# An eight-core transformer layer: tail transposes and half of the next layer norm issued ahead of the output projection

## The chip, the cores and the metric

The kernel runs on one Trainium2 chip, on all 8 of its cores at once, each core with one of the 8 sequences of the batch. No core speaks to another. The metric is the device time in microseconds (us) of the slowest core.

## What is computed

One layer with adaptive layer norms, on x of shape 8 x 2048 x 1024, 16 heads, and 8 experts:

```python
h = layernorm(x) * (1 + ca) + sa              # sa, ca, ga, sb, cb, gb come from silu(c) @ wmod
Q, K, V = h @ wq + bq, h @ wk + bk, h @ wv + bv
Q, K, V = (t.reshape(B * 16, 2048, 64) for t in (Q, K, V))
ctx = softmax(Q @ K.T / 8) @ V
out = ctx.reshape(B, S, E) @ wo + bo + h
x = x + ga * (layernorm(out) * gamma + beta)
h = layernorm(x) * (1 + cb) + sb
p = softmax(h @ gate_w + gate_b);  p = p * (p >= 0.1);  p = p / sum(p)
x = x + gb * sum_e p[:, e] * (h @ expert_w[e] + expert_b[e])
```

The reshape takes the heads from rows, not from columns: a head is made of 128 whole rows of the projections, so 256 rows hold two complete heads. Attention over them needs nothing of the other rows.

## The kernel before

The 2048 rows of a core are cut into 8 **octets** of 256 rows (two tiles of 128, i = 0 and 1). The loop at line 683 takes one octet after the other, and each is a fixed sequence that is written out by hand; every engine has one queue of instructions in order, and semaphores tie the queues together. In an octet come:

1. The rest of the first layer norm (lines 700 to 734). For each tile, VectorE turns the normalised rows that lie in `Kasm` into h: times CAb (L707), plus SAb (L710) in fp32 in `hf32`, and a bf16 copy into `h_bf` (L713). Then TensorE transposes the 8 blocks of 128 columns of `hf32` (L726) into two PSUM places of `pbD` in turn, and VectorE copies each to `hT` (L731). `hf32` holds one tile, so the second tile's h waits for the first one's transposes.
2. Q and K projections into `pbA` (L754), read out by VectorE into `Qasm` and `Kasm` (L764, L769), V projections into `pbB` and `pbC` (L804, read out by L812).
3. Attention (lines 827 to 953): four passes of 16 steps; a step is two score matmuls (L878), an exponential on ScalarE (L889), two matmuls with V (L851), and two matmuls whose result nobody reads (L897, L903). Between passes the context is scaled into `ctxFM` (L934, L939, L943). In the first three passes VectorE and ScalarE also run parts of the chain of the octet before (`chain_stage`: second and third layer norm), whose stage 4 leaves the first tile of h2 in `hf32`.
4. When the last pass is read out, GpSimd issues a transfer within SBUF that brings half of `ctxFM` to the lower 64 partitions (L949, the **context shift**), and behind it the load of the next octet's wq (L480). The output projection (L967, L974) waits for the shift: 36 matmuls, first into `pbA`, then into `pbB`. VectorE adds `h_bf` and writes `preLN` (L982).
5. The **tail** of the octet before (`emit_tail_transposes`, not in octet 0): 16 transposes of h2 (L598) with 16 copies to `h2T` (L605); between the 8th and the 9th, VectorE makes h2 of the second tile (L574, L578).
6. The **gate** of the octet before (`emit_gate_tail`): per tile, small matmuls (L623, L633, L674) and some 14 small VectorE instructions in a chain (L630 to L678).
7. The **first part of the next octet's layer norm** (`emit_ln1_pair`): statistics, two small ScalarE operations and the normalised rows into `Kasm` (L401 to L417), for both tiles; then the loads of the next weights are put in GpSimd's queue. The load into `wbuf1` waits for the output projection, which reads it.

Octet 0 has neither 5 nor 6, octet 7 has no 7. Behind the loop, the tail and the gate of octet 7 follow, then the experts. Semaphore `v1` counts VectorE's instructions, `t1`, `m1`, `m2` and `t2` count TensorE's; `pbd_guard` holds back the next octet's L897 until all of `v1` up to the octet's end is reached. A helper (`Prog.emit`) puts a drain ahead of each VectorE and ScalarE instruction that reads what the same engine has just written, or that counts a semaphore.

Of the kernel before, what the change touches and what calls it, by code (L numbers as in the profile page):

```python
# [13 lines left out]
BF16 = mybir.dt.bfloat16  # L14
# [6 lines left out]
DM = 1024  # L21
NB = 16
NOCT = 8
# [76 lines left out]
def build_program():  # L100
# [28 lines left out]
    CAb = sb("CAb", [128, DM], BF16)  # L129
    SAb = sb("SAb", [128, DM], BF16)  # L130
# [43 lines left out]
    P = Prog(nc, sems, None)  # L174

    for tt in range(NB):
        P.emit("sync", lambda e, tt=tt: e.dma_start(
            xsb[:, DM * tt:DM * (tt + 1)], x_h.ap()[128 * tt:128 * (tt + 1), :]),
            inc="dx", inc_n=16)
# [4 lines left out]
        inc="dsc", inc_n=16)  # L184
# [192 lines left out]
    h_bf = sb2("h_bf", [128, 2 * DM], BF16)  # L377
# [44 lines left out]
    ln1_sv = {}  # L422

# [11 lines left out]
    if True:  # L435
# [32 lines left out]
        emit_ln1_pair(0)  # L468
        P.flush_block()
# [19 lines left out]
    TAILT1 = {}  # L489
# [193 lines left out]
    for oct_ in range(NOCT):  # L683
        if True:
# [15 lines left out]
            for i in range(2):  # L700
                tt = 2 * oct_ + i
                hw = [ln1_sv[oct_][i]]
                if i == 0 and oct_ >= 2:
                    hw.append(("t1", TAILT1[oct_ - 2]))
                if i == 1:
                    hw.append(("t1", P.val("t1")))
                P.emit("vector", lambda e, i=i: e.tensor_mul(  # L707
                    hf32[:, 0:DM], Kasm[:, DM * i:DM * (i + 1)], CAb[:, :]),
                    waits=hw, writes=("hf",))
                P.emit("vector", lambda e, i=i: e.tensor_add(  # L710
                    hf32[:, 0:DM], hf32[:, 0:DM], SAb[:, :]),
                    reads=("hf",), writes=("hf",), inc="v1")
                P.emit("vector", lambda e, i=i: e.tensor_copy(  # L713
                    h_bf[:, DM * i:DM * (i + 1)], hf32[:, 0:DM]),
                    reads=("hf",), inc="v1")
                hdone_i = P.val("v1")
# [238 lines left out]
        if True:  # L955
            pso0 = pbA[:, :]
# [24 lines left out]
            for i in range(2):  # L981
                P.emit("vector", lambda e, i=i: e.tensor_add(  # L982
                    preLN[:, DM * i:DM * (i + 1)], pso[i][:, :],
                    h_bf[:, DM * i:DM * (i + 1)]),
                    waits=[("m2", m2v[i])], writes=("pl%d" % i,), inc="v1")
                PLV[(oct_, i)] = P.val("v1")
            if oct_ >= 1:
                emit_tail_transposes(oct_ - 1, recip_copied)
                emit_gate_tail(oct_ - 1)
            if oct_ + 1 < NOCT:  # L990
                emit_ln1_pair(oct_ + 1)
                load_weight(oct_ + 1, 0)
                load_weight(oct_ + 1, 1)
# [129 lines left out]
```

How the kernel before makes its waits and increments, by code:

```python
            def run(eng):  # L76
                for fn, waits, inc, inc_n in ops[eng_name]:
                    for s, v in waits:
                        eng.wait_ge(sems[s], v)
                    ins = fn(eng)
                    if inc is not None:
                        ins.then_inc(sems[inc], inc_n)
```

## Time and profile before

| | us |
|---|---|
| median of 3 runs | 2604.74 |
| lowest, highest | 2585.26, 2699.93 |
| profiled execution, its own time | 2597.9 |
| span of its slowest core (core 2) | 2596.4 |
| spans of the other cores | 2568.4 to 2588.5 |
| TensorE busy on core 2 | 1843.8 |
| VectorE busy on core 2 | 903.1 |
| mean granted TensorE clock, core 2 (share of 2.4 GHz) | 0.820 |

The span runs from the first to the last instruction of a core; the 1.5 us between it and the execution's own time lie around it. Octets lie between 318 and about 2048 us of the span, the experts behind 2100 us. Numbers with an L are lines of the kernel, names with an arrow are what an instruction writes and reads, and "idle before" names what ended the idle time of the engine ahead of a row. The granted clock is 0.50 at 1.2 GHz and 1.00 at 2.4 GHz.

### The profile page before, as it was taken

The numbers are of one execution on the slowest core, as the hardware profiler recorded it, in microseconds if no ns is written. First come the engines' busy times: TensorE is split into PE (matmuls) and PEld (weight loads), VectorE is DVE, ScalarE is ACT, GpSimd is POOL, SyncE is SP. The second block draws the span as 40 slices with busy tenths as digits, with TensorE's granted clock in tenths as the row PEclk, the third lists the DMA queues.
The fourth block names the chain that finished last, engine by engine and source line by source line (L and its number), as shares of the span: only waits on it lengthen the run. The fifth ranks groups of instructions, "written<-read, shape, count | busy, mean of one in ns | idle before, by whom it ended". The sixth has DMA issues, their size and how long they took to land.

```text
span 2596.4 us, 23765 instructions; the slowest of 8 cores (2568.4 to 2596.4 us)
## 1 busy us (share of the span) xinstructions
PE 1843.8 (71%) x7658; PEld 725.2 (28%) x7658; DVE 903.1 (35%) x1481; ACT 719.3 (28%) x692; POOL 42.4 (2%) x78
## 2 busy tenths in 40 slices
PE   0131189688668849948874993897588379999994
PEld 0000042242232223213222321422322124444441
DVE  2432130242262053134216214322620553333336
ACT  0000026327307504712640660363076000000000
POOL 0000000000000000000000000000000000000000
PEclk9855588789879868878886986978798569999997
DMA  8625730120120112012011101201200031112203
GB/s 235 194 89 95 187 115 1 69 74 1 69 73 1 37 35 71 1 69 73 1 56 54 34 1 69 73 1 69 73 1 4 1 66 33 33 33 51 47 1 130
DMA packets 41837, 150.48 MB, mean 58 GB/s; under 512 B 15597, under 2 KB 15597, under 8 KB 37112
## 3 DMA queue, kind: packets, MB, share of 16 engines
q0 software_dynamic: 20480, 96.51, 13.8%
q1 hardware_dynamic: 21240, 52.46, 6.3%
q8 instruction: 68, 1.11, 0.2%
q14 instruction: 49, 0.40, 0.1%
HBM read 151.09 MB, written 16.78 MB: 65 GB/s over the span
## 4 chain that ended last, share of the span: by engine, by line
PE 56%; DVE 12%; ACT 8%; issue 5%; DMA 4%; DVEq 2%; ACTq 1%; POOLq 0%; SPq 0%
PE pbA L1061 9%; PE pbC L851 9%; PE pbB L1061 9%; PE pbD L897 6%; PE pbA L878 5%; PE pbB L878 5%; ACT hT L889 4%; PE pbA L754 3%; PE pbD L903 2%; PE pbD L726 2%; PE pbA L967 2%; DVEq L54 2%; DMA Kasm<-Kasm 2%; DVE recipB L934 2%; ACT recipB L919 1%
## 5 line engine op out<-in xcount | busy, mean ns | idle before, releaser
L889 ACT ACTIVATE hT<-pbA,cm,c 128x1024 bf16<-128x1024 f32 x256 | 308.2, 1204 | 480.3 <-PE pbA L878 476.3
L851 PE MATMUL pbC<-hT,Vbuf 128*65 128x512 bf16 x1024 | 340.6, 418 | 39.6 <-ACT hT L889 37.7
L889 ACT ACTIVATE hT<-pbB,cm,c 128x1024 bf16<-128x1024 f32 x256 | 308.1, 1204 | 108.6 <-PE pbB L878 103.3
L934 DVE CAST recipB<-pbD 64x1024 bf16<-64x1024 f32 x32 | 38.9, 1216 | 812.5 <-PE pbD L929 812.5
L1061 PE MATMUL pbA<-We,h2T 128*128 128x512 bf16 x1024 | 234.2, 382 | 1.8 <-DVE facc L1034 1.8
L897 PE MATMUL pbD<-CAb 128*128 128x512 bf16 x512 | 217.9, 426 | 22.4 <-DVE recipB L934 22.4
L1061 PE MATMUL pbB<-We,h2T 128*128 128x512 bf16 x1024 | 231.5, 379 | 0.0
L878 PE MATMUL pbB<-Qasm,Kasm 64*128 64x512 bf16 x512 | 172.0, 420 | 0.0
L878 PE MATMUL pbA<-Qasm,Kasm 64*128 64x512 bf16 x512 | 169.2, 414 | 2.8 <-DMA Kasm<-Kasm 2.8
L754 PE MATMUL pbA<-hT,wbuf 128*128 128x256 bf16 x1024 | 145.2, 293 | 20.9 <-DVE Qasm L769 7.4
L903 PE MATMUL pbD<-CAb 128*128 128x256 bf16 x512 | 150.3, 294 | 0.0
L726 PE MATMUL pbD<-identf,hf 128*128 128x128 f32 x128 | 53.6, 444 | 129.6 <-DVE h_bf L713 120.8
L1061 PEld LDWEIGHTS pbA<-We,h2T 128*128 128x128 bf16 x1024 | 100.7, 98 | 125.4 <-issue 6.2
L1061 PEld LDWEIGHTS pbB<-We,h2T 128*128 128x128 bf16 x1024 | 100.1, 98 | 121.0
L851 PEld LDWEIGHTS pbC<-hT,Vbuf 128*65 128x65 bf16 x1024 | 104.6, 119 | 104.6 <-issue 79.9
L1069 DVE SCALAR_TENSOR_TENSOR facc<-pbA,w_gate,facc 128x1024 bf16<-128x1024 f32 x64 | 82.2, 1284 | 143.7 <-PE pbA L1061 143.7
L1069 DVE SCALAR_TENSOR_TENSOR facc<-pbB,w_gate,facc 128x1024 bf16<-128x1024 f32 x64 | 82.2, 1284 | 138.5 <-PE pbB L1061 138.5
L897 PEld LDWEIGHTS pbD<-CAb 128*128 128x128 bf16 x512 | 49.6, 97 | 272.2 <-issue 272.2
L283 PE MATMUL pbA<-macc,onescol 128*1 128x512 f32 x24 | 14.1, 720 | 153.1 <-DVEq L271 147.3
L754 PEld LDWEIGHTS pbA<-hT,wbuf 128*128 128x128 bf16 x1024 | 99.5, 104 | 66.7 <-issue 48.8
L598 PE MATMUL pbD<-identf,hf 128*128 128x128 f32 x128 | 46.5, 387 | 66.7 <-DVE hf L578 45.6
L646 ACT ACTIVATE gatee<-gatef,stats 128x8 f32<-128x8 f32 x16 | 4.8, 301 | 300.1 <-DVE stats L642 300.1
(162 smaller groups left out, 1468.2 us busy)
## 6 DMA issues: line engine op xcount, KB each, us to landing
wbuf<-wbh POOLq DMA_DIRECT2D x32, 2048.0 KB, 9.0
wmstage<-wmod SPq DMA_DIRECT2D x32, 768.0 KB, 4.9
We<-ew POOLq DMA_DIRECT2D x8, 2048.0 KB, 13.7
xsb<-x SPq DMA_DIRECT2D x16, 512.0 KB, 13.0
wbh<-wbuf SPq DMA_DIRECT2D x4, 2048.0 KB, 13.3
out<-xsb SPq DMA_DIRECT2D x16, 512.0 KB, 2.6
wbuf<-wq POOLq DMA_DIRECT2D x1, 2048.0 KB, 15.6
wbuf<-wk POOLq DMA_DIRECT2D x1, 2048.0 KB, 35.6
```

Of the source, the lines that this page charges most:

```text
L54: self.ops[eng].append((lambda e: e.drain(), (), None, 0))
L726: P.emit("tensor", lambda e, cch=cch, par=par: e.transpose(pst[par][:, :], hf32[:, 128 * cch:128 * (cch + 1)], identf[:, :]), waits=tw, in ...
L754: P.emit("tensor", lambda e, wtile=wtile, fo=fo, fc=fc, par=par: e.matmul(psq[par][:, :], wtile[:, DM * fc + 128 * fo:DM * fc + 128 * (fo ...
L851: P.emit("tensor", lambda e, h01=h01, gp=gp, q4=q4, par=par: e.matmul(psc[:, 512 * q4:512 * (q4 + 1)], vview[:, h01, gp, 0:65], PT[:, 1024 ...
L878: P.emit("tensor", lambda e, h01=h01, q2=q2, gp=gp, q4=q4, par=par: e.matmul(pss[par][:, 512 * q4:512 * (q4 + 1)], Kasm[0:64, T * h01 + 12 ...
L889: P.emit("scalar", lambda e, par=par: e.activation(PT[:, 1024 * par:1024 * (par + 1)], pss[par][:, :], AF.Exp, bias=cm3[:, :], scale=c0125 ...
L897: P.emit("tensor", lambda e: e.matmul(pbD[:, 0:512], CAb[:, 0:128], CAb[:, 0:512], start=True, stop=True), waits=fw)
L903: P.emit("tensor", lambda e: e.matmul(pbD[:, 0:256], CAb[:, 0:128], CAb[:, 0:256], start=True, stop=True), inc=("m1" if gp == 15 else None))
L934: P.emit("vector", lambda e: e.tensor_copy(recipB[0:64, :], psr[:, :]), waits=[("t2", tv)], writes=("recipB",), inc="v1")
L967: P.emit("tensor", lambda e, i=i, ec=ec, hh=hh: e.matmul(pso[i][:, 512 * hh:512 * (hh + 1)], cview[:, 0, ec, i, :], wbuf1[:, DM * ec + 512 ...
L1061: P.emit("tensor", lambda e, e_i=e_i, tt=tt, fc=fc, hh=hh, par=par: e.matmul(pse[par][:, 512 * hh:512 * (hh + 1)], h2T[:, T * fc + 128 * t ...
L1069: P.emit("vector", lambda e, e_i=e_i, tt=tt, par=par: e.scalar_tensor_tensor(facc[:, DM * tt:DM * (tt + 1)], pse[par][:, :], w_gate[:, NEX ...
```

## The change

Three things move, and nothing is added or dropped in number.

- The tail of the octet before (part 5) is issued ahead of the output projection instead of behind it, on TensorE and on VectorE.
- The first part of the next octet's layer norm (part 7) is issued behind the tail and ahead of the `preLN` additions.
- The h of the next octet's first tile (L707, L710, L713 for i = 0) leaves the start of the next octet. A new function, `emit_h0`, issues it directly behind the first part of the layer norm; for octet 0 it stands at the end of the block that prepares the weights. As it writes `h_bf` while the current octet's first tile there is still to be read, `h_bf` gets a third slot, and the first tile alternates between slots 0 and 2.

The gate (part 6) and the weight loads stay behind the `preLN` additions.

```diff
--- before.py
+++ after.py
@@ -374,7 +374,8 @@
     wbuf0 = sb2("wbuf0", [128, NFC * DM], BF16)
     wbuf1 = sb2("wbuf1", [128, NFC * DM], BF16)
     wbuf = (wbuf0, wbuf1)
-    h_bf = sb2("h_bf", [128, 2 * DM], BF16)
+    h_bf = sb2("h_bf", [128, 3 * DM], BF16)
+    h0slot = lambda o: (o % 2) * 2 * DM
     xnscr = sb2("xnscr", [128, 2 * DM], BF16)
     sqscr = xnscr
     preLN = sb2("preLN", [128, 2 * DM], BF16)
@@ -420,6 +421,22 @@
         return ("v1", P.val("v1"))
 
     ln1_sv = {}
+    HD0 = {}
+
+    def emit_h0(o, extra_t1=None):
+        hw = [ln1_sv[o][0]]
+        if extra_t1 is not None:
+            hw.append(("t1", extra_t1))
+        P.emit("vector", lambda e: e.tensor_mul(
+            hf32[:, 0:DM], Kasm[:, 0:DM], CAb[:, :]),
+            waits=hw, writes=("hf",))
+        P.emit("vector", lambda e: e.tensor_add(
+            hf32[:, 0:DM], hf32[:, 0:DM], SAb[:, :]),
+            reads=("hf",), writes=("hf",), inc="v1")
+        P.emit("vector", lambda e, o=o: e.tensor_copy(
+            h_bf[:, h0slot(o):h0slot(o) + DM], hf32[:, 0:DM]),
+            reads=("hf",), inc="v1")
+        HD0[o] = P.val("v1")
 
     def emit_ln1_pair(o):
         svs = []
@@ -466,6 +483,7 @@
         P.emit("vector", lambda e: e.tensor_copy(borow_bf[:, :], rowB[:, 0:DM]),
                reads=("rowBB",), inc="v1")
         emit_ln1_pair(0)
+        emit_h0(0)
         P.flush_block()
 
     slot_free = {0: None, 1: None}
@@ -699,21 +717,20 @@
             P.emit("vector", lambda e: e.memset(vview[:, :, :, 64:65], 1.0))
             for i in range(2):
                 tt = 2 * oct_ + i
-                hw = [ln1_sv[oct_][i]]
-                if i == 0 and oct_ >= 2:
-                    hw.append(("t1", TAILT1[oct_ - 2]))
                 if i == 1:
-                    hw.append(("t1", P.val("t1")))
-                P.emit("vector", lambda e, i=i: e.tensor_mul(
-                    hf32[:, 0:DM], Kasm[:, DM * i:DM * (i + 1)], CAb[:, :]),
-                    waits=hw, writes=("hf",))
-                P.emit("vector", lambda e, i=i: e.tensor_add(
-                    hf32[:, 0:DM], hf32[:, 0:DM], SAb[:, :]),
-                    reads=("hf",), writes=("hf",), inc="v1")
-                P.emit("vector", lambda e, i=i: e.tensor_copy(
-                    h_bf[:, DM * i:DM * (i + 1)], hf32[:, 0:DM]),
-                    reads=("hf",), inc="v1")
-                hdone_i = P.val("v1")
+                    hw = [ln1_sv[oct_][1], ("t1", P.val("t1"))]
+                    P.emit("vector", lambda e: e.tensor_mul(
+                        hf32[:, 0:DM], Kasm[:, DM:2 * DM], CAb[:, :]),
+                        waits=hw, writes=("hf",))
+                    P.emit("vector", lambda e: e.tensor_add(
+                        hf32[:, 0:DM], hf32[:, 0:DM], SAb[:, :]),
+                        reads=("hf",), writes=("hf",), inc="v1")
+                    P.emit("vector", lambda e: e.tensor_copy(
+                        h_bf[:, DM:2 * DM], hf32[:, 0:DM]),
+                        reads=("hf",), inc="v1")
+                    hdone_i = P.val("v1")
+                else:
+                    hdone_i = HD0[oct_]
                 ev0 = P.val("v1")
                 for cch in range(NFC):
                     k = i * NFC + cch
@@ -953,6 +970,12 @@
             V_EXP_LAST = exp_done[63]
 
         if True:
+            if oct_ >= 1:
+                emit_tail_transposes(oct_ - 1, recip_copied)
+            if oct_ + 1 < NOCT:
+                emit_ln1_pair(oct_ + 1)
+                emit_h0(oct_ + 1,
+                        extra_t1=(TAILT1[oct_ - 1] if oct_ >= 1 else None))
             pso0 = pbA[:, :]
             pso1 = pbB[:, :]
             pso = (pso0, pso1)
@@ -979,16 +1002,15 @@
                 m2v[i] = P.val("m2")
             slot_free[1] = ("m2", P.val("m2"))
             for i in range(2):
-                P.emit("vector", lambda e, i=i: e.tensor_add(
+                hcol = DM if i == 1 else h0slot(oct_)
+                P.emit("vector", lambda e, i=i, hcol=hcol: e.tensor_add(
                     preLN[:, DM * i:DM * (i + 1)], pso[i][:, :],
-                    h_bf[:, DM * i:DM * (i + 1)]),
+                    h_bf[:, hcol:hcol + DM]),
                     waits=[("m2", m2v[i])], writes=("pl%d" % i,), inc="v1")
                 PLV[(oct_, i)] = P.val("v1")
             if oct_ >= 1:
-                emit_tail_transposes(oct_ - 1, recip_copied)
                 emit_gate_tail(oct_ - 1)
             if oct_ + 1 < NOCT:
-                emit_ln1_pair(oct_ + 1)
                 load_weight(oct_ + 1, 0)
                 load_weight(oct_ + 1, 1)
             pbd_guard = P.val("v1")
```

On VectorE, at the end of octet 2, the queue before runs from the last context scaling (L943) to the gate's first copy (L630):

```order
L939 TENSOR_TENSOR ctxFM<-pbC,recipB 64x4x128
L943 TENSOR_TENSOR ctxFM<-pbC,recipB 64x4x128
L982 TENSOR_TENSOR preLN<-pbA,h_bf 128x1024
L982 TENSOR_TENSOR preLN<-pbB,h_bf 128x1024
L605 CAST h2T<-pbD 128x128 x8
L574 TENSOR_TENSOR hf<-xnscr,CBb 128x1024
L578 TENSOR_TENSOR hf<-hf,SBb 128x1024
L605 CAST h2T<-pbD 128x128 x8
L630 COPY gEM<-pbC 8x128
```

In the changed kernel (its line numbers are larger: L960 is the last scaling, L623 the copies to `h2T`, L592 and L596 h2) the same place goes on with the tail and the layer norm's statistics:

```order
L960 TENSOR_TENSOR ctxFM<-pbC,recipB 64x4x128
L623 CAST h2T<-pbD 128x128 x8
L592 TENSOR_TENSOR hf<-xnscr,CBb 128x1024
L596 TENSOR_TENSOR hf<-hf,SBb 128x1024
L623 CAST h2T<-pbD 128x128 x8
L402 BN_STATS stats<-xsb 128x6
```

Ten rows of the layer norm further on, VectorE comes to `emit_h0` (L430 to L436), to the `preLN` additions (L1006) and to the gate (L648):

```order
L418 TENSOR_SCALAR Kasm<-xsb,stats 128x1024
L430 TENSOR_TENSOR hf<-Kasm,CAb 128x1024
L433 TENSOR_TENSOR hf<-hf,SAb 128x1024
L436 CAST h_bf<-hf 128x1024
L1006 TENSOR_TENSOR preLN<-pbA,h_bf 128x1024
L1006 TENSOR_TENSOR preLN<-pbB,h_bf 128x1024
L648 COPY gEM<-pbC 8x128
```

So the additions, which stood first, now stand behind 31 instructions that do not need the output projection, and the gate follows them at once. At the border of two octets VectorE's queue before was:

```order
L417 TENSOR_SCALAR Kasm<-xsb,stats 128x1024
L699 MEMSET Vbuf 128x32
L707 TENSOR_TENSOR hf<-Kasm,CAb 128x1024
L710 TENSOR_TENSOR hf<-hf,SAb 128x1024
L713 CAST h_bf<-hf 128x1024
L731 CAST hT<-pbD 128x128 x8
```

and it is now, from the gate's last rows on:

```order
L687 TENSOR_SCALAR w_gate<-gatee,stats 128x8
L696 CAST wT_bf<-pbC 8x128
L717 MEMSET Vbuf 128x32
L748 CAST hT<-pbD 128x128 x8
L722 TENSOR_TENSOR hf<-Kasm,CAb 128x1024
```

Nothing stands any more between the gate and the copies of the first tile's transposes but a memset. On TensorE the end of an octet before was (L929 belongs to the attention, L967 and L974 are the output projection):

```order
L929 MATMUL pbD<-recipB,onesb 64x512 x2
L967 MATMUL pbA<-wbuf,ctxFM 128x512 x16
L974 MATMUL pbA<-borow_bf,ones1b 128x512 x2
L967 MATMUL pbB<-wbuf,ctxFM 128x512 x16
L974 MATMUL pbB<-borow_bf,ones1b 128x512 x2
L598 MATMUL pbD<-identf,hf 128x128 x16
L623 MATMUL pbC<-h2T,gw_bf 8x128 x8
```

and it is now (L946 is the attention's row, L616 the tail's transposes, L990 and L997 the output projection, L641 the gate's first matmuls):

```order
L946 MATMUL pbD<-recipB,onesb 64x512 x2
L616 MATMUL pbD<-identf,hf 128x128 x16
L990 MATMUL pbA<-wbuf,ctxFM 128x512 x16
L997 MATMUL pbA<-borow_bf,ones1b 128x512 x2
L990 MATMUL pbB<-wbuf,ctxFM 128x512 x16
L997 MATMUL pbB<-borow_bf,ones1b 128x512 x2
L641 MATMUL pbC<-h2T,gw_bf 8x128 x8
```

The 16 transposes now stand between the attention and the output projection. On ScalarE the two small operations per tile of the layer norm now come ahead of the gate's two exponentials. The queues of GpSimd and SyncE keep their order.

## Rows read from the trace of the kernel before

**Rows 1.** Part 1 of the page: busy us, share of the span, instructions.
```profile
PE 1843.8 (71%) x7658; PEld 725.2 (28%) x7658; DVE 903.1 (35%) x1481; ACT 719.3 (28%) x692; POOL 42.4 (2%) x78
```

**Rows 2.** Timeline of core 2, 898 to 962 us: start, length, engine, line, names, count, idle before.
```profile
897.84 0.68 DVE L943 TENSOR_TENSOR ctxFM<-pbC,recipB 64x512 bf16<-64x512 f32 x1
...
902.34 6.26 PE L967 MATMUL pbA<-wbuf,ctxFM 128*128 128x512 bf16 x16 [6.67 <-DMA ctxFM<-ctxFM]
...
909.06 3.63 PE L967 MATMUL pbB<-wbuf,ctxFM 128*128 128x512 bf16 x16
...
913.33 1.22 DVE L982 TENSOR_TENSOR preLN<-pbB,h_bf 128x1024 bf16<-128x1024 f32 x1 [2.87 <-PE pbB L974]
914.71 0.29 DVE L605 CAST h2T<-pbD 128x128 bf16<-128x128 f32 x1 [0.16 <-issue]
...
925.08 0.29 DVE L605 CAST h2T<-pbD 128x128 bf16<-128x128 f32 x1 [0.17 <-PE pbD L598]
926.74 0.28 DVE L630 COPY gEM<-pbC 8x128 f32<-8x128 f32 x1 [1.37 <-PE pbC L623]
...
937.89 0.28 DVE L678 CAST wT_bf<-pbC 8x128 bf16<-8x128 f32 x1 [0.62 <-PE pbC L674]
938.09 0.67 DVE L401 BATCH_NORM_STATS2 stats<-xsb 128x6 f32<-128x512 f32 x1
...
944.11 0.81 DVE L417 TENSOR_SCALAR Kasm<-xsb,stats 128x1024 bf16<-128x1024 f32 x1
...
947.51 0.69 DVE L713 CAST h_bf<-hf 128x1024 bf16<-128x1024 f32 x1
948.91 0.29 DVE L731 CAST hT<-pbD 128x128 bf16<-128x128 f32 x1 [0.70 <-PE pbD L726]
...
952.33 0.29 DVE L731 CAST hT<-pbD 128x128 bf16<-128x128 f32 x1 [0.16 <-PE pbD L726]
...
960.72 1.65 PE L754 MATMUL pbA<-hT,wbuf 128*128 128x256 bf16 x7 [0.76 <-DVE hT L731]
```

**Rows 3.** Stretches of core 2: length; busy PE, PEld, DVE, ACT, POOL; clock; DMA share; GB/s.
```profile
898.50:902.30 3.80, 0.00 (x0) 0.00 (x0) 0.02 (x1) 0.00 (x0) 1.08 (x2) 0.50 0.60 129
913.20:925.50 12.30, 5.54 (x17) 2.39 (x16) 8.34 (x19) 0.00 (x0) 0.53 (x1) 0.69 0.47 172
```

**Rows 4.** Timeline of core 2, weight loads of the output projection.
```profile
903.14 0.15 PEld L967 LDWEIGHTS pbA<-wbuf,ctxFM 128*128 128x128 bf16 x1 [0.28 <-issue]
903.57 0.15 PEld L967 LDWEIGHTS pbA<-wbuf,ctxFM 128*128 128x128 bf16 x1 [0.28 <-issue]
```

**Rows 5.** Timeline of core 2's VectorE, end of octet 0 and start of octet 1.
```profile
491.00 0.68 DVE L943 TENSOR_TENSOR ctxFM<-pbC,recipB 64x512 bf16<-64x512 f32 x1
...
502.75 1.22 DVE L982 TENSOR_TENSOR preLN<-pbA,h_bf 128x1024 bf16<-128x1024 f32 x1 [11.06 <-PE pbA L974]
...
506.84 1.22 DVE L982 TENSOR_TENSOR preLN<-pbB,h_bf 128x1024 bf16<-128x1024 f32 x1 [2.87 <-PE pbB L974]
...
518.81 0.29 DVE L731 CAST hT<-pbD 128x128 bf16<-128x128 f32 x1 [0.70 <-PE pbD L726]
```

**Rows 6.** Timeline of core 2's VectorE in octet 7.
```profile
2007.10 0.68 DVE L943 TENSOR_TENSOR ctxFM<-pbC,recipB 64x512 bf16<-64x512 f32 x1
...
2036.39 0.28 DVE L630 COPY gEM<-pbC 8x128 f32<-8x128 f32 x1 [1.37 <-PE pbC L623]
```

**Rows 7.** Stretches of core 0: attention of octet 0, then of octet 5.
```profile
368.10:486.30 118.20, 103.29 (x417) 35.23 (x424) 10.32 (x12) 87.00 (x73) 0.00 (x0) 0.96 0.00 1
1426.70:1559.10 132.40, 117.02 (x416) 36.18 (x424) 23.83 (x34) 87.63 (x80) 0.00 (x0) 0.84 0.00 1
```

**Rows 8.** Answer for line 949, the context shift.
```profile
DMA to landing us min/median/max: 2.8/2.9/3.4
```

**Rows 9.** Answer for line 480, the weight loads from scratch.
```profile
DMA to landing us min/median/max: 7.9/9.0/14.0
```

## The prediction

> **What bounds the kernel now.** I read the page's busy times first. No engine fills the span: TensorE is busy 71% of it, VectorE 35%, ScalarE 28% [rows 1]. So the time is a chain through several engines, and the question is which stretches are serial. The list of cores came next (all within 28 us, clocks 0.820 to 0.832): every core tells the same story. Then I took the timeline of one border between two octets, from the last context scaling of octet 2 to the first Q projection of octet 3 [rows 2]. It lasts from 898.52 (897.84 + 0.68) to 960.72, that is 62.2 us, and it is one chain:
>
> - 3.8 us in which TensorE and VectorE stand, until the context shift lands at 902.3 [rows 2, 3];
> - the output projection and the last `preLN` addition, to 914.55;
> - the tail, first copy 914.71, last copy ending 925.37: 10.66 us;
> - the gate, to 938.17: 11.43 us from its first copy at 926.74, ahead of which TensorE's first gate matmuls take 1.37 us;
> - the layer norm's first part, 938.09 to 944.92: 6.83 us;
> - h of the first tile, to 948.20: 3.28 us;
> - eight transposes and their copies, 948.91 to 952.62: 3.71 us;
> - the same for the second tile (h, then transposes), 8.10 us to 960.72.
>
> In each item one engine waits for the other. Nothing of the next octet's attention can start before it ends, so every microsecond taken from this chain is a microsecond of the run. The border stands seven times in the program, six times in this form (octets 1 to 6) and once without tail and gate (octet 0); octet 7 has the projection, the tail and the gate.
>
> **Octets 1 to 6, step by step.** I count t from the end of the last scaling (898.52 before). The tail needs only octet-old data: h2 of its first tile has been in `hf32` since the third attention pass.
>
> 1. VectorE copies the tail's blocks out from t = 0.16 on, and is through at 0.16 + 10.66 = 10.8. TensorE's last transpose ends some 0.4 us earlier, at 10.4. The shift still lands at 3.8, under this work, so its wait vanishes; but the projection, which began at 3.8, now begins at 10.4.
> 2. The projection took from 902.34 to 913.2, 10.9 us [rows 2]: its `pbA` half took 6.26 us with the clock at first at 1.2 GHz, its `pbB` half 3.63 us at 2.4. I keep 10.9, as the clock was at 0.50 behind the attention [rows 3] and will be again, so it ends at 21.3.
> 3. Beside it VectorE does the layer norm's first part, 10.8 + 6.83 + some 0.1 = 17.7, and h of the first tile, 17.7 + 3.28 = 21.0. Both `preLN` additions follow (1.22 us and a gap each): 23.6. The second one could have started at 21.4, so VectorE is the later by 0.9 us. This is the new bound of the step, and it is nearly a tie.
> 4. The gate's first matmuls run on TensorE behind the projection, from 21.3 to 22.5, under the additions. The gate then needs its 11.43 us from 23.7: 35.1.
> 5. The transposes of the next first tile wait for nothing more than TensorE. The copies begin at 35.3 and take 3.71: 39.0. The rest is unchanged, 8.1: 47.1.
>
> The gain is 62.2 - 47.1 = 15.1 us at each of six borders, 90.6. It is less than the 6.83 + 3.28 + 10.66 us that move, since the projection lost its early start: what really vanishes is the shift's 3.8 us and the overlap of two 10 us pieces.
>
> **Octet 0.** There the projection begins when it did. VectorE's 10.1 us of layer norm and h fit in front of the first addition, which came 11.1 us after the last scaling (502.75 against 491.68) and can come there still [rows 5]. From the end of the second addition (508.06) to the first copy of the next transposes (518.81) stand 10.75 us [rows 5], of which a gap of 0.16 stays: gain 10.6.
>
> **Octet 7.** From the last scaling (2007.78) to the gate's first copy (2036.39) are 28.6 us [rows 6]. After: projection from 10.4 to 21.3, second addition to 22.7 (no layer norm holds VectorE), copy at 22.8. Gain 5.8. The gate and all behind it stay.
>
> **The start.** h of tile 0 moves ahead of a barrier between blocks instead of behind it, on the same chain; the weight loads leave the barrier with only 3.71 + 8.10 = 11.8 us of transposes and h [rows 2] between them and the first Q matmul. The median load takes 9.0 us, the slowest 14.0 [rows 9], and the one that Q reads is the first of the two. Zero, at worst 2.2 us.
>
> **Sum.** 90.6 + 10.6 + 5.8 = 107.0 us. Against the profiled execution, 2597.9 - 107.0 = 2490.9. The median shown is 2604.74, 7 us above it, and the lowest run 2585.26, 13 us below; I stay with 2491.
>
> What is nothing in this sum, and its cover: the third slot of `h_bf` is only an address. The load into `wbuf1` is issued when the projection ends, 10 us later against the shift, at t = 21.8; with 14.0 us for the slowest [rows 9] it lands at 36, and the K projection that reads it comes some 10 us after 47. If it took twice as long, the wait would still be none. The attention's own work is untouched.
>
> The cost that the trace does not show is VectorE's copies running while the shift is issued by GpSimd. Lower bound nothing; upper bound the 9.0 us that the large loads need in place of the shift's 2.9 [rows 8, 9], so 6.1 us later. At octets 1 to 7 the projection has 6.6 us of slack behind the shift and takes nothing; at octet 0 it costs at most 6.1. I take zero, as the shift's own row is the nearer one.
>
> The Trainium skill ("SBUF — State Buffer", section "Who interferes with whom") has a rule that speaks against this: a transfer issued by GpSimd waits for its descriptors while VectorE runs in a two-port mode, which copies and tensor_scalar between SBUF tiles can take. The tail's copies read PSUM and by the same page do not, so by this rule only octet 0, where the layer norm runs beside the shift, could lose. No run here shows it yet.
>
> **Rivals.**
>
> *The projection runs at 1.2 GHz throughout.* For it: beside the tail's transposes the clock fell to a mean of 0.69 before [rows 3], and sparse transposes now stand right ahead of it. Against: the projection also started at 1.2 GHz before, and rose within its own first half. Price: weight loads 0.43 us apart [rows 4], so 36 matmuls take 15.4 us and end at 25.8 in place of 21.3; second addition 27.1 against 23.6, 3.5 us at six borders, and 4.5 each at octets 0 and 7: 30 us. Time 2521. Were it at 2.4 GHz from the start, nothing would be gained, VectorE being later already.
>
> *The shift or VectorE pieces stretch under overlap*, 1 to 2 us at each of seven borders: 2500 to 2505. It is within my likeliest range.
>
> *The attention takes the time back, and the kernel is slower.* This is the other side. The attention's 64 steps took 118.2 us at clock 0.96 and 132.4 us at 0.84, on one core, with the same work [rows 7]: 1.18 us per hundredth of clock. The clock fell at different places in different octets, so it hangs on something not fixed by the program. With the quiet border cut from 62 to 47 us, the chip rests less, and if that kept the clock down, all eight attentions would pay. To eat 107 us, each must lose 13.4 us, so 0.11 of clock: from a mean near 0.89 to below 0.78, past the worst one seen. Beyond that point the kernel is slower, some 2610. Half of it (0.83) costs 8 x 7 = 57 us and ends at 2548, the case of "no change". Against: octet 0, with its short border, is followed by attentions like the others. More likely is redistribution: single attentions 5 us up or down, which moves the slowest core's sum by some 10 us either way.
>
> *The change does not do what it says*: that would need a wait which keeps the tail behind the projection. Its waits are h2 (from the third pass) and the last copy of `recipB`, which precedes the scaling. I give it no more than the rest of "no change".
>
> **Chances.** The forecast, with the redistribution, 2475 to 2506: 0.74. Projection at 1.2 GHz, 2507 to 2530: 0.14. A partly lower attention clock, 2531 to 2550: 0.05, most of it short of 2%. The far end, slower: 0.02. Below 2475: 0.05. A measurement of this kernel tells about 2% from no change, some 52 us. The range 2472 to 2526 leaves out the last cases. Faster 0.93, within 2% 0.05, slower 0.02.
>
> **What would show it right or wrong.** In the timeline of octets 2 and 3, the span from the last scaling to the first Q matmul should be 47 us, in octet 0 28.5. The projection's idle time should no longer be ended by the transfer but by the tail's last copies. Between the last tail copy and the first `preLN` addition VectorE should stand only for ScalarE's two small operations per tile. The first addition should start at about t = 21 and the gate's first copy at 23.7. If that copy comes at 27, the first rival holds. If all borders fit and the sum does not, the eight attentions must have grown, and their clock must be lower. If the projection still starts on the landing of the shift, at t above 10, the overlap slowed the transfer.

## The result, and the profile after

The changed kernel takes 2494.94 us (median of 9 runs), against 2590.41 us for the kernel before (median of 10, those of the table above among them). The ratio is 0.961, with a 95% interval of 0.9581 to 0.9639: faster by 3.6 to 4.2%, on 2590 us some 101 us. The medians themselves differ by 95.5 us, since in some executions of both kernels the cores of one die were granted a lower clock and took longer, and the medians include these while the ratio does not. The forecast was 2491 us, range 2472 to 2526.

The profiled execution took 2490.04 us. Its slowest core is core 7, with a span of 2488.5 us. Part 1 of its page, the counterpart of [rows 1]:

```profile
PE 1829.5 (74%) x7658; PEld 719.6 (29%) x7658; DVE 903.3 (36%) x1481; ACT 720.9 (29%) x692; POOL 42.4 (2%) x78
```

The counts are those of before and the busy times nearly so (TensorE 1829.5 us for 1843.8, VectorE 903.3 for 903.1); what has shrunk is the idle time between them. Where it went is in the timeline of core 7 at the end of octet 2, the counterpart of [rows 2] (start, length, engine, line, names; L960 is the last context scaling, L623 the tail's copies, L990 and L997 the output projection, L436 the end of h of the next first tile, L1006 the additions, L648 to L696 the gate, L748 the copies of the next transposes, L771 the first Q matmul):

```profile
889.40 0.68 DVE L960 TENSOR_TENSOR ctxFM<-pbC,recipB 64x512 bf16<-64x512 f32 x1
890.24 0.29 DVE L623 CAST h2T<-pbD 128x128 bf16<-128x128 f32 x1 [0.16 <-issue]
...
900.71 5.39 PE L990 MATMUL pbA<-wbuf,ctxFM 128*128 128x512 bf16 x16
900.90 0.29 DVE L623 CAST h2T<-pbD 128x128 bf16<-128x128 f32 x1 [0.17 <-PE pbD L616]
...
906.57 3.63 PE L990 MATMUL pbB<-wbuf,ctxFM 128*128 128x512 bf16 x16
...
910.13 0.60 PE L997 MATMUL pbB<-borow_bf,ones1b 1*128 1x512 bf16 x2
910.49 0.69 DVE L436 CAST h_bf<-hf 128x1024 bf16<-128x1024 f32 x1
911.35 1.22 DVE L1006 TENSOR_TENSOR preLN<-pbA,h_bf 128x1024 bf16<-128x1024 f32 x1 [0.16 <-PE pbC L641]
912.73 1.22 DVE L1006 TENSOR_TENSOR preLN<-pbB,h_bf 128x1024 bf16<-128x1024 f32 x1 [0.16 <-issue]
914.11 0.28 DVE L648 COPY gEM<-pbC 8x128 f32<-8x128 f32 x1 [0.16 <-issue]
...
925.55 0.28 DVE L696 CAST wT_bf<-pbC 8x128 bf16<-8x128 f32 x1 [0.62 <-PE pbC L692]
...
926.12 0.29 DVE L748 CAST hT<-pbD 128x128 bf16<-128x128 f32 x1
...
929.54 0.29 DVE L748 CAST hT<-pbD 128x128 bf16<-128x128 f32 x1 [0.16 <-PE pbD L743]
...
937.95 4.25 PE L771 MATMUL pbA<-hT,wbuf 128*128 128x256 bf16 x20 [0.79 <-DVE hT L748]
```

The border runs from 890.08 to 937.95, 47.9 us in place of 62.2. The tail's first copy comes 0.16 us behind the last scaling. The projection starts at t = 10.6 (900.71), behind the tail's last transpose. VectorE goes through layer norm and h to 911.18, and both additions follow with 0.16 us ahead of each. The projection's last matmul had ended at 910.73, 2.0 us before the second addition started. So VectorE, not the projection, sets when the gate starts (914.11, t = 24.0). The gate's last copy ends at 925.83, and the next transposes' copies begin 0.3 us later.

How VectorE and TensorE now lie side by side is in two stretches of that border (length; busy PE, PEld, DVE, ACT, POOL; clock; DMA share; GB/s), the tail and the projection:

```profile
890.08:900.70 10.62, 5.92 (x14) 2.51 (x15) 6.78 (x18) 0.00 (x0) 1.08 (x2) 0.53 0.65 222
900.70:911.20 10.50, 10.50 (x45) 4.00 (x44) 8.13 (x15) 1.18 (x4) 0.00 (x0) 0.83 0.01 2
```

Before, TensorE and VectorE had no work in the 3.8 us under the shift [rows 3], and VectorE did one addition during the projection. Now VectorE is busy 8.13 of the 10.50 us of the second stretch.

The summary of what the projection's matmuls (L990) waited for says the same in one line:

```profile
  DMA ctxFM<-ctxFM: 6.7, 1
```

The shift ends the wait once, at octet 0. The same line of the kernel before named it 8 times, with 54.1 us. And the additions (L1006) wait for the projection at few places only:

```profile
  PE pbB L997: 5.5, 3
  PE pbA L997: 5.1, 1
```

The one for `pbA` is octet 7's, where no layer norm stands ahead; of the 5.5 us for `pbB`, 2.87 are octet 7's and 2.45 octet 0's. Before, all 16 additions waited, 106.6 us in sum. Octet 0's border on VectorE, counterpart of [rows 5]:

```profile
493.73 0.68 DVE L960 TENSOR_TENSOR ctxFM<-pbC,recipB 64x512 bf16<-64x512 f32 x1
...
508.24 1.22 DVE L1006 TENSOR_TENSOR preLN<-pbB,h_bf 128x1024 bf16<-128x1024 f32 x1 [2.45 <-PE pbB L997]
...
509.75 0.29 DVE L748 CAST hT<-pbD 128x128 bf16<-128x128 f32 x1
```

Second addition to first copy: 0.29 us in place of 10.75. And octet 7, counterpart of [rows 6]:

```profile
1907.22 0.68 DVE L960 TENSOR_TENSOR ctxFM<-pbC,recipB 64x512 bf16<-64x512 f32 x1
...
1929.87 0.28 DVE L648 COPY gEM<-pbC 8x128 f32<-8x128 f32 x1 [0.16 <-issue]
```

From the last scaling (1907.90) to the gate's first copy are 22.0 us in place of 28.6; on the mean of the cores 22.1 in place of 28.5.

### The profile page after: what moved, and what is told of

Read it like the earlier page. It is cut to its first block, busy times and chain, and to the rows that moved or that the text cites. A ratio compares the mean times of both kernels' runs of the same rounds, so it can differ in the third digit from the quotient of the medians.

```text
span 2488.5 us, 23765 instructions; the slowest of 8 cores (2440.9 to 2488.5 us)
## 1 busy us (share of the span) xinstructions
PE 1829.5 (74%) x7658; PEld 719.6 (29%) x7658; DVE 903.3 (36%) x1481; ACT 720.9 (29%) x692; POOL 42.4 (2%) x78
## 4 chain that ended last, share of the span: by engine, by line
PE 56%; DVE 12%; ACT 9%; issue 5%; DMA 3%; DVEq 2%; ACTq 1%; POOLq 0%; SPq 0%
PE pbA L1083 9%; PE pbB L1083 9%; PE pbC L868 8%; ACT hT L906 6%; PE pbD L914 5%; PE pbA L895 5%; PE pbB L895 4%; PE pbA L771 3%; DMA wbuf<-wbh 3%; PE pbD L920 2%; PE pbD L616 2%; PE pbD L743 2%; DVE recipB L951 2%; DVEq L54 1%; ACT recipB L936 1%
## 5 line engine op out<-in xcount | busy, mean ns | idle before, releaser
L771 PE MATMUL pbA<-hT,wbuf 128*128 128x256 bf16 x1024 | 145.0, 293 | 20.4 <-DVE Qasm L786 6.6
L868 PEld LDWEIGHTS pbC<-hT,Vbuf 128*65 128x65 bf16 x1024 | 101.2, 117 | 107.4 <-issue 81.4
L771 PEld LDWEIGHTS pbA<-hT,wbuf 128*128 128x128 bf16 x1024 | 99.4, 104 | 66.2 <-issue 48.9
L616 PE MATMUL pbD<-identf,hf 128*128 128x128 f32 x128 | 51.6, 427 | 73.3 <-DVE hf L596 45.2
## 6 DMA issues: line engine op xcount, KB each, us to landing
wbuf<-wk POOLq DMA_DIRECT2D x1, 2048.0 KB, 36.4
```

Source lines behind the costliest of these rows:

```text
L616: P.emit("tensor", lambda e, cch=cch, tpar=tpar: e.transpose(pstcB[tpar][:, :], hf32[:, 128 * cch:128 * (cch + 1)], identf[:, :]), waits=f ...
L771: P.emit("tensor", lambda e, wtile=wtile, fo=fo, fc=fc, par=par: e.matmul(psq[par][:, :], wtile[:, DM * fc + 128 * fo:DM * fc + 128 * (fo ...
L868: P.emit("tensor", lambda e, h01=h01, gp=gp, q4=q4, par=par: e.matmul(psc[:, 512 * q4:512 * (q4 + 1)], vview[:, h01, gp, 0:65], PT[:, 1024 ...
```

## The experiments

Each edit is against the changed kernel unless it says otherwise. Times are medians; ratios are to the kernel before on the same chip (2601 us for the first four, 2600 for the others), so the ratio compares better than the time. A "border" is the time from the last context scaling to the next octet's first Q matmul.

**Parts of the change.** The first two runs each leave one of the moved pieces where it was. The tail alone:

```diff
-            if oct_ + 1 < NOCT:
-                emit_ln1_pair(oct_ + 1)
-                emit_h0(oct_ + 1,
-                        extra_t1=(TAILT1[oct_ - 1] if oct_ >= 1 else None))
             pso0 = pbA[:, :]
...
             if oct_ + 1 < NOCT:
+                emit_ln1_pair(oct_ + 1)
+                emit_h0(oct_ + 1,
+                        extra_t1=(TAILT1[oct_ - 1] if oct_ >= 1 else None))
                 load_weight(oct_ + 1, 0)
```

> Only the tail stands ahead of the output projection; the layer norm's first part and h of the next first tile are back behind the gate. Theory A (the border is one chain, and each piece is worth what it takes off that chain): per border, t from the last context scaling, tail to 11.1, projection from 10.7 to 20.3, second addition to 21.6, gate to 33.5, layer norm and h to 43.7, first Q matmul at 56.3 against 62.2 before and 47.9 in the changed kernel. 5.9 us at six borders, nothing at octet 0, 5.8 at octet 7: 41 us, so some 2549 us. Theory B (the gain comes from filling TensorE's idle time ahead of the projection, with the clock that goes with it; the layer norm's place matters little): most of the 95 us is there already, some 2505 to 2515 us.

Measured: 2557.35 us, ratio 0.9827 (0.9792 to 0.9862), which on 2590 us is 45 us less. Octet 2's border on its slowest core, last scaling and first Q matmul, is 56.8 us, and the 48 borders of octets 1 to 6 on all cores lie between 55.3 and 56.9:

```profile
907.59 0.68 DVE L960 TENSOR_TENSOR ctxFM<-pbC,recipB 64x512 bf16<-64x512 f32 x1
...
965.04 3.36 PE L771 MATMUL pbA<-hT,wbuf 128*128 128x256 bf16 x15 [0.76 <-DVE hT L748]
```

Theory A had 56.3 and 41 us. The borders themselves scatter less than the times: summed over octets 0 to 6 they are 36.4 us shorter than before on the mean of the cores, and octet 7's piece is 6.2 us shorter, 42.6 us together, of 103.1 in the changed kernel. Filling TensorE's idle time ahead of the projection is less than half of the gain; B, which had 2505 to 2515 us, falls.

The layer norm alone, with h of the next first tile between the tail and the gate:

```diff
-            if oct_ >= 1:
-                emit_tail_transposes(oct_ - 1, recip_copied)
             if oct_ + 1 < NOCT:
                 emit_ln1_pair(oct_ + 1)
-                emit_h0(oct_ + 1,
-                        extra_t1=(TAILT1[oct_ - 1] if oct_ >= 1 else None))
+                if oct_ == 0:
+                    emit_h0(1)
...
             if oct_ >= 1:
+                emit_tail_transposes(oct_ - 1, recip_copied)
+                if oct_ + 1 < NOCT:
+                    emit_h0(oct_ + 1, extra_t1=TAILT1[oct_ - 1])
                 emit_gate_tail(oct_ - 1)
```

> The layer norm's first part stands ahead of the additions, the tail behind them as before, h of the next first tile behind the tail (hf32 is taken until then). Theory A: layer norm to 7.0, projection 3.8 to 14.7, second addition to 16.0, tail to 26.9, h to 30.2, gate to 42.0, first Q matmul at 54.1 against 62.2 before. 8.1 us at six borders, 10.6 at octet 0, nothing at octet 7: 59 us, some 2531 us. Octet 0's border must be as in the changed kernel, 27 to 28 us. Theory B: TensorE still stands 6.7 us ahead of the projection, so nearly nothing but octet 0: some 2575 to 2580 us.

Measured: median 2558.51 us, ratio 0.974 (0.9691 to 0.9789), 67 us on 2590; the forecast was 59. Octet 2's border on core 6, whose mean granted clock was 0.832 (cores 0 to 3 of this execution had 0.815 to 0.817):

```profile
891.34 0.68 DVE L960 TENSOR_TENSOR ctxFM<-pbC,recipB 64x512 bf16<-64x512 f32 x1
...
945.94 3.36 PE L771 MATMUL pbA<-hT,wbuf 128*128 128x256 bf16 x15 [0.76 <-DVE hT L748]
```

53.9 us, and 52.7 to 54.7 on cores 4 to 7 (52.7 to 55.4 on all), for 54.1 forecast. Octet 0's is 27.2 to 28.4, as in the changed kernel. By the ratios the two parts give 45 and 67 us, 112 together, and the change 101, with intervals of 9 to 13 us to either side. The borders are sharper: the layer norm's place takes 60.6 us off those of octets 0 to 6 on the mean of the cores (61.2 on cores 4 to 7) and nothing off octet 7's piece, the tail's place 42.6 off both, together 103 to 104, and the change takes off 103.1. The two parts add up.

**What moving h is worth.** h of the next first tile behind the gate:

```diff
                 emit_ln1_pair(oct_ + 1)
-                emit_h0(oct_ + 1,
-                        extra_t1=(TAILT1[oct_ - 1] if oct_ >= 1 else None))
             pso0 = pbA[:, :]
...
             if oct_ + 1 < NOCT:
+                emit_h0(oct_ + 1,
+                        extra_t1=(TAILT1[oct_ - 1] if oct_ >= 1 else None))
                 load_weight(oct_ + 1, 0)
```

> As the changed kernel, but h of the next first tile stands behind the gate. Theory A: without it the additions wait for the projection (first addition from 18.0, second from 20.4 to 21.6), the gate ends at 33.5, h at 36.9, first Q matmul at 49.4 against 47.9: 1.5 us at six borders and 3 at octet 0, some 12 us slower than the changed kernel, so 2507 us. Rival (moving h is worth its own 3.3 us at each of seven borders): 23 us slower, 2518 us.

Measured: 2510.49 us, ratio 0.9657 (0.9619 to 0.9695), 12 us above the changed kernel's ratio on 2590. As the intervals of the two ratios overlap, the border decides:

```profile
899.30 0.68 DVE L960 TENSOR_TENSOR ctxFM<-pbC,recipB 64x512 bf16<-64x512 f32 x1
...
949.62 3.36 PE L771 MATMUL pbA<-hT,wbuf 128*128 128x256 bf16 x15 [0.75 <-DVE hT L748]
```

49.6 us here, 48.6 to 50.6 on all cores against 47.5 to 48.2, and octet 0's 30.8 to 32.0 against 27.1 to 28.1. In the changed kernel the border's length did not follow the projection, which took 8.5 to 10.3 us (from its first matmul to the last of L990): over the 48 borders of octets 1 to 6 a projection longer by 1 us went with a border longer by 0.0 us, while here it went with 0.9 us, since VectorE reaches the additions first. So h moved is worth 1.5 us of its 3.3 at these borders, as Theory A had it, and 3.8 at octet 0, for 3 forecast.

**The shift's wait.** The context shift is issued a second time, first in the kernel before as a control, then in the changed kernel:

```diff
                 waits=[("v1", evac_done), ("dsh", P.val("dsh"))], inc="dsh", inc_n=16)
+            P.emit("gpsimd", lambda e: e.dma_start(
+                cview[64:128, 0, :, :, :], cview[0:64, 1, :, :, :]),
+                waits=[("v1", evac_done), ("dsh", P.val("dsh"))], inc="dsh", inc_n=16)
             V_DSH_CTX = P.val("dsh")
```

> The kernel before with the context shift issued a second time behind the landing of the first, the projection waiting for both. It is the control of the next run. The shift is exposed there, so each of the 8 octets should grow by the second shift's issue and landing, 3.5 to 4 us: the projection starts at some 7.7 us behind the last scaling instead of 3.8, the borders read 66 in place of 62.2, and the time grows by 28 to 32 us.

> The changed kernel with the same second shift. Theory A (the shift lies under the tail with 6.6 us to spare from octet 1 on): the projection still starts at 10.6 to 10.9, the borders stay at 47.8 us, only octet 0's grows, by 4 us; time within 5 us of the changed kernel, ratio to before 0.961 to 0.964. Rival (VectorE's copies beside GpSimd's issue slow the transfers, so that the first shift already takes most of the tail's time): the projection starts 2 us or more later at each octet, 10 to 30 us in all.

Measured: the control takes 2625.1 us, ratio 1.0103 (1.0073 to 1.0133), 27 us more, just under the 28 to 32 expected. Its projection starts at t = 7.2 to 7.7 and its borders read 64.4 to 66.5. Its matmuls of the projection (L970) waited for the shift at all eight octets:

```profile
  DMA ctxFM<-ctxFM: 80.5, 8
```

In the changed kernel the median is 2506.06 us and the ratio 0.9637 (0.9594 to 0.9681), not to be told from 0.961. The projection's (L993) wait for the shift:

```profile
  DMA ctxFM<-ctxFM: 10.2, 1
```

Once, at octet 0, whose border grew from 27.6 to 30.7 us on the mean of the cores, 3.1 us for some 4 expected; the others stayed at 47.4 to 48.3. The shift is fully hidden from octet 1 on, with room for another. That GpSimd issues it beside VectorE's copies costs nothing that its landings in the changed kernel would show, against [rows 8]:

```profile
DMA to landing us min/median/max: 2.9/2.9/3.3
```

By the Trainium skill ("SBUF — State Buffer", section "Who interferes with whom") a copy with one input in SBUF contends with GpSimd only in a two-port mode. The conditions of that mode are on another page; by the Trainium skill ("VectorE: DVE Perf Modes", section "Why PSUM operands drop a tier") an operand in PSUM rules it out. So no delay was to be expected from the tail's copies, which read PSUM; the trace agrees. In octet 0, where the layer norm runs beside the shift and where the prediction allowed a loss, the shift landed after 2.9 us on all eight cores too, and the projection started 3.8 to 4.2 us behind the last scaling, as before. On core 7 VectorE ran the layer norm's statistics (L404) while GpSimd issued the shift (495.04 to 495.56), and its first tensor_scalar (L418) only from 496.99. So no run shows what a two-port instruction during that issue would cost.

**A higher clock for the projection.** Fourteen matmuls whose result nobody reads fill TensorE's idle places in the tail of octets 1 to 7:

```diff
+        if co < NOCT - 1:
+            for n in range(6):
+                P.emit("tensor", lambda e: e.matmul(
+                    pbB[:, 0:512], CAb[:, 0:128], CAb[:, 0:512],
+                    start=True, stop=True),
+                    waits=([("s1", V_EXP_LAST)] if n == 0 else []))
         for gp in range(16):
...
                 emit_h2(co, 1, ("t1", tail_t1[7]))
+                if co < NOCT - 1:
+                    for _ in range(8):
+                        P.emit("tensor", lambda e: e.matmul(
+                            pbB[:, 0:512], CAb[:, 0:128], CAb[:, 0:512],
+                            start=True, stop=True))
```

> The changed kernel with 14 matmuls of 512 columns whose result nobody reads in TensorE's idle places of the tail (6 ahead of the first transpose, 8 while VectorE makes h2 of the second tile), in octets 1 to 7, to keep the clock at 2.4 GHz for the projection. Theory A (VectorE is the later at the additions by about 1 us): the projection falls from 8.4 to 10.3 us to about 8, the additions don't start earlier, the borders stay at 47.8, the time within 5 us of the changed kernel. Rival (the projection's clock still sets the border): borders 1 to 2 us shorter, 8 to 14 us in all.

Measured: 2492.94 us, ratio 0.96 (0.9572 to 0.9627), no difference from the changed kernel. But the edit did not do what it was made for: the projection took 7.7 us three times and else 8.8 to 10.3, as in the changed kernel. Stretches of core 6 at the end of octet 2: the tail in two pieces, then the projection's first 3.2 us:

```profile
888.00:892.00 4.00, 3.25 (x10) 1.44 (x11) 2.80 (x8) 0.00 (x0) 1.07 (x2) 0.76 0.69 164
892.00:896.80 4.80, 3.79 (x12) 1.42 (x10) 3.26 (x8) 0.00 (x0) 0.00 (x0) 0.84 0.92 338
896.80:900.00 3.20, 3.05 (x8) 1.05 (x8) 2.15 (x6) 0.41 (x2) 0.00 (x0) 0.52 0.08 31
```

TensorE was busy 3.25 of 4.00 and 3.79 of 4.80 us in the tail, the clock went up and down, and the projection still began at 0.52. The borders are 0.4 us shorter, and part of the tail's transposes ran at 2.4 GHz. So this run does not test whether a faster projection would help. The evidence that it would not is the changed kernel itself: borders of 47.5 to 48.2 us with projections of 8.5 to 10.3 us, and no tie between the two.

**Taking more out of the border.** If the border is the chain that counts, its next piece is the gate's 11.8 us. In the next run the gate of octets 0 to 5 is cut into eight pieces (per tile: matmuls and copy, transpose and maximum, exponential and weights, transpose and copy), issued between steps of the last attention pass two octets later, in `pbD`'s upper bank, with the end of the pass held until VectorE has read it:

```diff
+    GSLOT = {1: (0, 0), 3: (0, 1), 5: (0, 2), 7: (0, 3),
+             8: (1, 0), 10: (1, 1), 12: (1, 2), 14: (1, 3)}
...
+                    if oct_ >= 2 and seg == 3 and gp in GSLOT:
+                        gate_piece(2 * (oct_ - 2) + GSLOT[gp][0], *GSLOT[gp])
                     pend = (k, seg)
...
                         if seg > 0:
-                            tw.append(("v1", recip_copied))
+                            tw.append(("v1", P.val("v1") if seg == 3 else recip_copied))
...
-            if oct_ >= 1:
+            if oct_ == NOCT - 1:
                 emit_gate_tail(oct_ - 1)
```

> As the changed kernel, but the gate of octets 0 to 5 is taken out of the border and issued in eight pieces between the steps of the last attention pass of two octets later. Theory A: the border falls by the gate's 11.8 us to 36.1 us at octets 1 to 6, 71 us; TensorE gets 3.2 us more at most in each of six attentions and ScalarE 0.6, 4 to 20 us in all: some 2430 to 2445 us. Rival (the attention gives the time back, by waits of TensorE on VectorE between steps or by a lower clock after shorter borders): attentions longer by 5 to 12 us each, 2465 to 2495 us.

Measured: 2435.61 us, ratio 0.9377 (0.9347 to 0.9407). Octet 2's border:

```profile
877.92 0.68 DVE L1019 TENSOR_TENSOR ctxFM<-pbC,recipB 64x512 bf16<-64x512 f32 x1
...
914.80 3.27 PE L828 MATMUL pbA<-hT,wbuf 128*128 128x256 bf16 x15 [0.76 <-DVE hT L805]
```

36.2 us; all 48 borders of octets 1 to 6 lie between 35.8 and 36.4, for 36.1 forecast. The eight attentions of a core, from the first score matmul to the last scaling, took 1006 us in sum on the mean of the cores, against 983 in the changed kernel: 23 us, where Theory A had 4 to 20. Of these, 2.6 us lie in the attentions of octets 0 and 1, which got no gate; the six others are longer by 20.5 us, 3.4 each. In the profiled executions whose attention is as before, the changed kernel's among them, the sum is 980 to 992 us, so part of the 23 us can be such scatter. The rival, 5 to 12 us for each attention and 2465 us or more in all, falls.

The last run also moves the tail itself: its 16 transposes stand one by one between steps of the third and fourth pass (each waits for the copy before it, as both use one PSUM bank), and the gate's pieces in the first pass:

```diff
+                    if oct_ >= 2 and seg == 0 and gp in GSLOT:
+                        gate_piece(2 * (oct_ - 2) + GSLOT[gp][0], *GSLOT[gp])
+                    if oct_ >= 1 and seg == 2 and gp >= 7 and gp <= 14:
+                        tail_piece(oct_ - 1, gp - 7)
+                    if oct_ >= 1 and seg == 3 and gp == 1:
+                        emit_h2(oct_ - 1, 1, ("t1", tail_st[oct_ - 1]["t1"][7]))
+                    if oct_ >= 1 and seg == 3 and gp >= 5 and gp <= 12:
+                        tail_piece(oct_ - 1, gp + 3)
                     pend = (k, seg)
...
-                        if seg > 0:
-                            tw.append(("v1", recip_copied))
+                        if seg > 0 or oct_ >= 2:
+                            tw.append(("v1", P.val("v1")))
...
-            if oct_ >= 1:
-                emit_tail_transposes(oct_ - 1, recip_copied)
             if oct_ + 1 < NOCT:
                 emit_ln1_pair(oct_ + 1)
```

> The gate in the first attention pass of two octets later, and the tail itself between steps of the third and fourth pass of its own octet, so that a border has only the layer norm, h, the projection and the additions. Theory A: borders of octets 1 to 6 as octet 0's, 27.5 us against 36.1 with the gate alone taken out: 51 us, and some 8 us at octet 7; TensorE gets 16 fp32 transposes more in each of seven attentions, 3 to 8 us each: 20 to 56 us back. Some 2395 to 2430 us against 2435. Rival (what sits in the attention costs as much as at the border, since the steps there are full): 2435 us or more.

Measured: 2395.16 us, ratio 0.9219 (0.919 to 0.9249), the fastest kernel of this study, 7.8% below the one before. Octet 2's border:

```profile
872.25 0.68 DVE L1051 TENSOR_TENSOR ctxFM<-pbC,recipB 64x512 bf16<-64x512 f32 x1
...
900.98 3.36 PE L854 MATMUL pbA<-hT,wbuf 128*128 128x256 bf16 x15 [0.76 <-DVE hT L831]
```

28.0 us, all cores 26.7 to 29.0 from octet 1 to 6, for 27.5 forecast. Octet 7's piece is 6 us shorter than with the gate alone taken out, for 8 forecast. The attentions sum to 1012 us, 29 more than in the changed kernel, 4.1 for each of seven, though they now hold both the tail and the gate. What cost some 20 us at a border (47.8 against 27.9 on the mean) costs 4 between the steps of an attention. VectorE is mostly idle there (busy 23.83 of 132.40 us in [rows 7]); TensorE is not (117.02 us), and which part of the 4 us is its added work and which its waits is not shown.

## Why the prediction was right, point by point

**The border as one chain.** Right. Each of six kernels with another order at the border came out within 0.8 us of the border that the addition of row durations gave: 56.3, 54.1, 49.4, 47.1, 36.1 and 27.5 us forecast; 56.1, 53.8, 49.3, 47.8, 36.1 and 27.9 measured, on the mean of cores and of octets 1 to 6. Only the 47.1 was worked out before the changed kernel's trace was seen; the five others took their durations from it.

**The terms.** At octets 1 to 6 the border is 47.8 us on the mean, and 47.9 in the one shown, where 47.1 was worked out. There the tail ends at 11.1 us for 10.8: its first half had a granted clock of 0.95 before and has 0.58 now. Of these 0.3 us, 0.1 is left when h is done (21.1 for 21.0). The additions add some 0.2 (they end at 23.9 for 23.6, as the forecast left out one of the gaps of 0.16 us), the gate 0.3 (11.7 for 11.4), and the rest 0.1. At octet 0 it is 27.1 to 28.1 where 28.5 was worked out, at octet 7 22.0 where 22.8 was. Summed over octets 0 to 6, a core's borders fell from 411.3 to 314.6 us on the mean of the cores: 96.7 us, for 101.2 forecast; with octet 7's 6.4, 103 for 107. The 101 us by the ratio is near that sum. The spans of the two profiled executions differ by more, 116 us on the mean of the cores and 108 on the slowest: of the 116, 103 are these borders and octet 7's piece, 7 the attentions, 3 the time up to the first Q matmul, and 3 lie elsewhere. What is beyond the 103 is smaller than the scatter between the cores of one execution (2441 to 2489 us here), and nothing ties it to the change.

**VectorE as the new bound of step 3, by 0.9 us.** Right, and by more: its additions start 0.16 us behind h, the second one 2.0 us behind the projection's end on the mean of octets 1 to 6 (1.1 to 2.9), as most projections took less than the 10.9 us kept. The border does not move with the projection's length. The run with h behind the gate shows the other side: there the second addition always starts 0.1 us behind the projection's end.

**The time itself.** The forecast, 2490.9 us, lies 4 us below the median of 2494.94, and that nearness is in part luck. The execution it started from was 7.5 us above the pooled median of 2590.41, and the gain of 107.0 us was too large: by 4 us against the borders, by 6 against the 101 us of the ratio, by 11.5 against the 95.5 us between the medians. The two errors take each other back in part.

**The rivals.** *Projection at 1.2 GHz throughout*: didn't happen. It started at 1.2 GHz and rose within its first half as before, and took 10.0 us here, the last two matmuls (L997) included, for 10.9 in [rows 2]. *The shift slowed by VectorE*: fell, by the landings and the doubled shift. *The attention takes the time back*: fell. Shorter borders went with a higher mean clock, not a lower one. The two dies read 0.827 each before; after, and in the last run:

```profile
die 0 (median of its cores): 2468.5 us, clock 0.844
die 1 (median of its cores): 2470.6 us, clock 0.844
```

```profile
die 0 (median of its cores): 2386.8 us, clock 0.864
die 1 (median of its cores): 2376.4 us, clock 0.865
```

Part of that rise is only that the border, at a low clock (0.58 before and 0.61 after in the border of octet 2), is a smaller share of the span. But in the attentions alone the sum was 990 us before and 983 after, at a mean granted clock of 0.915 and 0.924 (the forecast had reckoned with some 0.89). The scatter the forecast spoke of is there: on single cores the sum is 961 to 998 us, and it was 978 to 1006 before.

**The weight loads and the start.** Right. No Q or K matmul (L771) waited for a load on any core; in the border shown, the first one (937.95) follows the last copy. What does wait for a load, in both kernels, are the V matmuls, 7.7 us per core before and after. The first Q matmul of the program comes at 334.8 us on the mean of the cores, against 338.2 before: no loss at the start.

## What to carry to other kernels

Where engines hand one another small pieces in turn, look for the longest such stretch, write its rows down as one chain, and recompute the chain for the new order: who is free when, and which of two engines comes later at each meeting. What a move is worth is what it takes from that chain, which may be less than its own length (h: 1.5 of 3.3 us). And a serial chain costs least where another stage keeps the busy engine fed: tail and gate together cost 20 us at a border and 4 inside an attention.

## What the runs showed of the hardware that was not expected

In the run with fourteen matmuls more, TensorE was busy 81 and 79% of the time in the two pieces of the tail (3.25 of 4.00 and 3.79 of 4.80 us, fp32 transposes and 512-column matmuls mixed), and the granted clock was still only 0.76 and 0.84 there, so in part at 1.2 GHz, and 0.52 as the projection began. Here the busy microseconds of a stretch did not tell what clock would be granted behind it. Why is open; no run here separates the transposes from the short pauses between them.
